# First attention's last blocks routed one by one, scatters spread, score weights multiplied ahead, experts' fetches reordered and tied to TensorE

## The reference, cut to what matters

```python
x = x + L0_xattn(layernorm(x), ctx, ctx, tokens, mask, ...)   # 16 heads, masked by equal tokens
x = x + L0_ffn(layernorm(x), router_w, w1, w2, expert_scale)  # top 2 of 8, silu
x = x + L1_xattn(layernorm(x), ctx, ...)                      # two directions, gated
x = x + L1_ffn(layernorm(x), Wg, bg, W1, W2, W3)              # top 2 of 8, capacity
```

## Time and profile before

| | |
|---|---|
| median of 3 runs | 1492.52 us (1490.99 to 1493.09) |
| the profiled execution's own time | 1491.39 us |
| its span, first to last instruction | 1489.5 us |
| mean granted TensorE clock | 0.957 of full |
| TensorE busy | 1356.2 us (91%) |
| VectorE / ScalarE / POOL busy | 850.7 / 817.5 / 667.9 us |
| first attention, TensorE's last count | 392 us |
| first experts, first matmul to last | 413.9 to 821.2 us |

### The profile page before, as it was taken

How to read it: one execution, slowest core, us unless ns; L and a number is a source line. 1 busy time by engine, 2 the same in 40 slices (tenths; PEclk the granted TensorE clock), 3 DMA queues, 4 the chain that set the end, 5 groups by cost and what they waited for, 6 DMA issues and landing times.

```text
span 1489.5 us, 37452 instructions
## 1 busy us (share of the span) xinstructions
PE 1356.2 (91%) x12922; PEld 1106.6 (74%) x12922; DVE 850.7 (57%) x2352; ACT 817.5 (55%) x1907; POOL 667.9 (45%) x936
## 2 busy tenths in 40 slices
PE   6999999997369999999999699999993999999996
PEld 5777777775226666666666699999982999999996
DVE  4787778887523222332232377777774566666664
ACT  4787777775135555554554355555552554454443
POOL 3234554554553333333310447777756444444322
PEclk8999999999579999999999899999996999999998
DMA  4343433432049999998897133333313433443331
GB/s 136 98 123 94 119 101 96 121 89 52 22 101 171 188 213 182 173 179 159 150 167 156 57 97 90 87 90 94 88 59 79 128 118 115 131 125 106 123 116 52
DMA packets 280856, 172.97 MB, mean 116 GB/s; under 512 B 212990, under 2 KB 259296, under 8 KB 280676
## 3 DMA queue, kind: packets, MB, share of 16 engines
q1 hardware_dynamic: 257940, 134.79, 39.7%
q0 software_dynamic: 18608, 32.21, 8.1%
q10 hardware_dynamic: 4128, 3.57, 0.9%
HBM read 93.44 MB, written 31.97 MB: 84 GB/s over the span
## 4 chain that ended last, share of the span: by engine, by line
PE 61%; DMA 3%; issue 3%; DVE 2%; ACT 2%; POOL 1%; another core or an unknown queue 1%; DVEq 0%; ACTq 0%; POOLq 0%; SPq 0%
PE psum L2308 14%; PE psum L1345 12%; PE psum L1358 12%; PE psum L2324 7%; PE psum L1828 4%; PE psum L1909 3%; PE psum L1834 3%; PE psum L1899 2%; DMA b_hT<-b_h 2%; PE psum L1875 1%; PE psum L1878 1%; DMA c_yg<-dram_expert_rows,c_gi 1%; ACT c_prT L1759 1%; PE psum L2292 1%
## 5 line engine op out<-in xcount | busy, mean ns | idle before, releaser
L1276 DVE SCALAR_TENSOR_TENSOR b_h<-b_hid,b_h 128x1024 f16<-128x1024 f32 x71 | 87.0, 1226 | 282.1 <-ACT b_h L1308 276.2
L2308 PE MATMUL psum<-d_xT,d_w 128*128 128x256 f16 (+1 forms) x2304 | 228.7, 256 | 0.0
L1345 PE MATMUL psum<-arena,b_xT 128*128 x852 | 200.8, 387 | 23.0 <-DMA b_xT<-b_x 21.6
L1358 PE MATMUL psum<-arena,b_hT 128*128 x1704 | 202.3, 276 | 13.1 <-DMA b_hT<-b_h 10.3
L2308 PEld LDWEIGHTS psum<-d_xT,d_w 128*128 128x128 f16 x2304 | 199.5, 98 | 19.3
L1358 PEld LDWEIGHTS psum<-arena,b_hT 128*128 128x128 f16 x1704 | 167.4, 99 | 52.2 <-issue 18.1
L1345 PEld LDWEIGHTS psum<-arena,b_xT 128*128 128x128 f16 x852 | 84.7, 100 | 114.9 <-issue 32.7
L1186 POOL DMA_INDIRECT b_xg<-dram_normed,b_gi x71 | 67.3, 948 | 207.4 <-DVE b_x L1269 195.6
L1303 ACT ACTIVATE b_hid<-psum 128x512 f32<-128x512 f32 x142 | 84.6, 597 | 137.5 <-PE psum L1345 99.2
L2368 ACT ACTIVATE d_sg<-psum 128x256 f32<-128x256 f32 (+1 forms) x192 | 65.9, 348 | 142.9 <-PE psum L2308 137.8
L2426 DVE SCALAR_TENSOR_TENSOR d_hf<-psum,d_sg 128x256 f32<-128x256 f32 (+1 forms) x192 | 71.2, 379 | 102.1 <-ACT d_sg L2368 86.1
(11 more groups left out here) (320 smaller groups left out, 2942.8 us busy)
## 6 DMA issues: line engine op xcount, KB each, us to landing
d_wst<-in_L_w SPq DMA_DIRECT2D x64, 384.0 KB
stage<-in_L_w SPq DMA_DIRECT2D x32, 512.0 KB
dram_expert_rows<-b_ys SPq DMA_DIRECT2D x71, 128.0 KB
ctxT<-in_ctxT SPq DMA_DIRECT2D x64, 128.0 KB
dram_normed<-xn SPq DMA_DIRECT2D x64, 128.0 KB
x<-in_x SPq DMA_DIRECT2D x32, 128.0 KB, 4.8
dram_x<-xnew SPq DMA_DIRECT2D x32, 128.0 KB
c_x<-dram_x SPq DMA_DIRECT2D x32, 128.0 KB
```

Of the source, the lines that this page charges most:

```text
L1276: dve.scalar_tensor_tensor(out=h16[:, p, 1, :], in0=hid[:, p, :], scalar=H_SCALE, in1=h16[:, p, 0, :], op0=ALU.mult, op1=ALU.subtract).the ...
L1345: i = pe.matmul(psum[:, 1 + 2 * p + half, :], xT[:, j % NT, px, c, :], weights(e, c, pw, half * 512, 512), start=(n == 0), stop=(n == len( ...
L1358: i = pe.matmul(psum[:, 6 + p, 0:D], hT[:, p, ph_, c, :], weights(e, 2 + c // 4, pw, (c % 4) * D, D), start=(n == 0), stop=(n == len(terms ...
L2308: i = pe.matmul(psum[:, q, m * n:(m + 1) * n], w16[:, fc % RING, pw, col:col + P], xT[:, p, px, c, at:at + n], start=(k == 0), stop=(k == ...
```

## The change

1. **Routing of the last blocks.** `GROUPS` ends in two groups of 2 (blocks 24 to 27) and four groups of 1 (28 to 31). The counts of these four go to another PSUM bank (`count_bank`). Their two factors (`probability`, `weights_out`) are made for all four at once (`WGROUPS`), after `tables`. In steps after 32 `slots_out` stands ahead of `top`.
2. **Scatters.** `scattered_at` gives 4 scatters to steps 30, 31 and 32 of POOL's loop where 3, 3 and 2 stood, and 2 each to steps 33, 34 and 35 where 2, 2, 2 and, in step 36, 4 stood.
3. **The fold** leaves the first experts. Its weights come by SP in the first attention; TensorE turns them in steps 32, 33 and 34 of the first attention (`turn_pe`), ScalarE copies them out (`turn_act`), and both multiply them between the two stages (`fold_pe`, `fold_act`). The results that second attention adds to its own weights are copied there by POOL (`scaled`), for which TensorE and VectorE wait at that stage's start (`c_cast`).
4. **Fetches.** POOL's loop of the first experts calls `gather(j)` ahead of `load_ids(j + 2)`, and `gather(j)` from j = 6 on also waits until `down(j - 6)` is done.
5. **Silu.** One `activation` of one column with Silu stands ahead of ScalarE's loop of the first experts.

```diff
-            GROUPS = [(b, RG) for b in range(0, NB - 2 * RG, RG)] + [(b, 2) for b in range(NB - 2 * RG, NB, 2)]
+            GROUPS = [(b, RG) for b in range(0, NB - 2 * RG, RG)] + [(b, 2) for b in range(NB - 2 * RG, NB - RG, 2)]
+            SINGLE = len(GROUPS)
+            WGROUPS = GROUPS + [(NB - RG, RG)]
+            GROUPS = GROUPS + [(b, 1) for b in range(NB - RG, NB)]
...
                     if n == RG and b < NB - 3 * RG:
                         return b + RG + 4
-                    if b < NB - 6:
-                        return NB - 4 + (2 * (b - NB + 3 * RG) + k) // 3
-                    return min(b + 6, NB + 4)
+                    if b < NB - 5:
+                        i = 2 * (b - NB + 3 * RG) + k
+                        return NB - 4 + (i // 3 if i < 6 else 2 + (i - 6) // 4)
+                    return min(b + 5, NB) if b < NB - RG else b + 4
...
+        def turn_pe(pe, k):
+            if k == 0:
+                pe.wait_ge(f_ld, 16 * (len(WN) + len(BN)))
+            t, bank = score_w[WN[k]], 3 + k
+            for o in range(DC):
+                for c in range(DC):
+                    i = pe.transpose(psum[:, bank, o * D + c * P:o * D + (c + 1) * P], t[:, c, o * P:(o + 1) * P], ident[:, :])
+            i.then_inc(turn_done, 1)
...
+            pe.wait_ge(turn_out, 2)
+            product(w["Wq_c"], w["Wk_s"], 3)
+            pe.wait_ge(turn_out, 4)
+            product(w["Wq_s"], w["Wk_c"], 4)
+            column(0, w["Wk_c"], bqs)
+            column(2, w["Wk_s"], bqc)
+            column(4, w["Wq_c"], bks)
+            column(6, w["Wq_s"], bkc)
+            dot(8, bqc, bks)
+            dot(9, bqs, bkc).then_inc(col_done, 1)
+
+        def fold_act(act):
+            act.wait_ge(col_done, 1)
+            act.activation(bm[:, :, :].rearrange("p d c -> p (d c)"), psum[:, 2, 0:4], ACT.Copy, scale=SC)
+            act.activation(consts[:, :], psum[:, 2, 4:10], ACT.Copy, scale=SC).then_inc(col_out, 1)
+            for k, t in enumerate((mc, ms)):
+                act.wait_ge(fold_done, k + 1)
+                act.activation(flat(t), psum[:, 3 + k, :], ACT.Copy).then_inc(fold_out, 1)
...
                 def gather(j):
                     if inside(j):
                         if due(j - NX + 1):
                             pool.wait_ge(xlo_ready, j - NX + 1)
+                            pool.wait_ge(down_done, j - NX + 1)
...
                 for j in range(N_B):
+                    gather(j)
                     load_ids(j + 2)
-                    gather(j)
...
+                act.activation(hid[:, 0, 0:1], xn2T[:, 0, 0:1], ACT.Silu)
                 for j in range(-4, N_B + 2):
...
             def scaled(pool):
                 pool.wait_ge(c_const, 16 * NL)
+                pool.wait_ge(col_out, 1)
+                for k, wt in enumerate((wvc, wvs)):
+                    pool.tensor_copy(wt[:, :, D:D + 1].rearrange("p c a -> p (c a)"), consts[:, 2 * k:2 * k + 2])
+                pool.tensor_copy(bv[:, :, D:D + 1].rearrange("p d a -> p (d a)"), consts[:, 4:6])
...
             @block.scalar
             def _(act):
                 a_act(act)
-                b_act(act, c_weights, c_fold_act)
+                fold_act(act)
+                b_act(act, c_weights)
...
             @block.tensor
             def _(pe):
                 a_pe(pe)
-                b_pe(pe, c_fold_pe)
+                fold_pe(pe)
+                b_pe(pe)
```

More of the change, by code:

```diff
@@ L207, in build @@
         x3_st, row_st = load_sems("x3_st"), sem("row_st")
-        kept = len(owned)
+        A_WORK = 61184
+        beside, in_wq = region(SHARED + WEIGHTS + A_WORK, WORK - A_WORK), region(SHARED + WEIGHTS + STAGED, 2048)
+        WN = ("Wq_c", "Wk_s", "Wq_s", "Wk_c")
+        BN = ("bqc", "bks", "bqs", "bkc")
+        score_w = {n: (in_wq if n == "Wk_c" else beside)("c_" + n, [P, DC, D]) for n in ("Wq_c", "Wq_s", "Wk_s", "Wk_c")}
+        score_b = beside("c_bqk", [P, len(BN), DC])
+        bm, consts = beside("c_bm", [P, 2, DC]), beside("c_consts", [P, 6])
@@ new lines, in build @@
+        f_ld, turn_done, turn_out, col_done, col_out, fold_done, fold_out = sem("f_load"), *(psem(f"f_{n}") for n in (
+            "turn", "turno", "col", "colo", "fold", "foldo"))
+        kept = len(owned)
+        SC = D ** -0.5
+        flat = lambda t: t[:, :, :].rearrange("p c d -> p (c d)")
+        bqc, bks, bqs, bkc = (score_b[:, i, :] for i in range(len(BN)))
+        mc, ms = score_w["Wq_c"], score_w["Wq_s"]
+        def turn_pe(pe, k):
[6 more added lines that the diff above has]
+            i.then_inc(turn_done, 1)
@@ new lines, in turn_act, with fold_pe, column, dot @@
+        def turn_act(act, k):
+            act.wait_ge(turn_done, k + 1)
+            act.activation(flat(score_w[WN[k]]), psum[:, 3 + k, :], ACT.Copy).then_inc(turn_out, 1)
+        def fold_pe(pe):
+            w = score_w
+            def column(at, wt, bias):
+                for k in range(DC):
+                    for o in range(DC):
+                        pe.matmul(psum[:, 2, at + k:at + k + 1], wt[:, o, k * P:(k + 1) * P], bias[:, o:o + 1], start=(o == 0), stop=(o == DC - 1))
+            def dot(at, x, y):
+                for o in range(DC):
+                    i = pe.matmul(psum[:, 2, at:at + 1], x[:, o:o + 1].to_broadcast([P, P]), y[:, o:o + 1], start=(o == 0), stop=(o == DC - 1))
+                return i
+            def product(wq, wk, bank):
+                for k in range(DC):
+                    for o in range(DC):
+                        i = pe.matmul(psum[:, bank, k * D:(k + 1) * D], wq[:, o, k * P:(k + 1) * P], wk[:, o, :], start=(o == 0), stop=(o == DC - 1))
+                i.then_inc(fold_done, 1)
+            pe.wait_ge(turn_out, 2)
[8 more added lines that the diff above has]
+            dot(9, bqs, bkc).then_inc(col_done, 1)
@@ L311, in last_of, with weights_of, place, count_bank @@
                 return g if j == n - 1 else None
+            def weights_of(b):
+                if b == NB - 1:
+                    return SINGLE
+                return last_of(b) if b < NB - RG else None
+            def place(g):
+                first, n = GROUPS[g]
+                o = max(0, g - SINGLE)
+                return o, o + n, min(g, SINGLE)
+            def count_bank(g):
+                return 0 if g >= SINGLE else 1
             def scattered(g, p):
@@ L863, in count @@
                     for j in range(n):
-                        i = pe.matmul(psum[:, 1, tot:tot + E], ones16[:, :], ghots16[:, j, :], start=(j == 0), stop=(j == n - 1))
+                        i = pe.matmul(psum[:, bank, tot:tot + E], ones16[:, :], ghots16[:, at + j, :], start=(j == 0), stop=(j == n - 1))
                     i.then_inc(cnt_done, 1)
@@ L985, in top @@
                         g, j, n = group_of[b]
+                        at, _, older = place(g)
                         if b == 0:
@@ L1262, in of_slots, with b_dve @@
                 dve.wait_ge(t_steps, k.next())
-            def b_dve(dve, fold):
+            def b_dve(dve):
                 def low_x(j):
@@ L1364, in b_pe @@
                     down(j - 1)
-                    fold(pe, j)
             def b_sync(sp, first_rows):
@@ L1453, in second_attention @@
             c_const, c_cast = sem("c_const"), psem("c_cast")
-            turn_done, turn_out, col_done, col_out, fold_done, fold_out = (psem(f"c_{n}") for n in ("turn", "turno", "col", "colo", "fold", "foldo"))
             yg_ld, x_ld, ctx_ld = load_sems("c_gather"), [sem(f"c_row{i}") for i in range(6)], load_sems("c_ctx")
```

250 lines of the change are left out of this document (99 added, 151 removed).

## The result

The changed kernel takes 1469.28 us (median of 4 runs, 1463.9 to 1472.17) against 1492.8 us (4 runs, 1490.99 to 1499.34): ratio 0.9837, 95% interval 0.9814 to 0.986, so 23.5 us less in the medians. The forecast was 1466.9, with a range of 1461 to 1478. The profiled execution took 1469.38 us (span 1467.6, granted clock 0.965), 22.0 us less than that of before.

The account below looks back on a forecast made before the run. TensorE was taken to bound the experts' steady part, waits the step into it. Gains 11.2 + 4.4 + 10.0 = 25.6 us from 1491.39 gave 1465.8, plus 1.1 for the median: 1466.9 us, range 1461 to 1478.

Parts of the forecast that it names:

- the hold: Behind up(0) in the first experts: ScalarE's 9.20 us wait without known releaser, expected to go with a shorter fetch run.
- the pieces put at nothing: Start to block 0's pT, attention blocks 0 to 31, and down(70) to the end: each forecast at 0.
- The fold leaves the experts: First experts' steady part: removing the fold's matmuls and the clock drop behind them saves 11.2 us.
- The matmuls' 9.45: First experts: the fold's turnings, bias groups and products take 9.45 us on TensorE's chain.
- the clock's 1.72: First experts: the up behind the longest bias group takes 4.31 us instead of 2.59, put down to one-column matmuls.
- The fold's new place: End of first attention and gap before up(0): fold hidden in waits, cost 0; ScalarE free at 405.6, deciding up(0).
- Routing and first fetch: Step from first attention into experts: earlier scatters, ids and rows; up(0) starts 4.4 us earlier, at 409.5.
- From `up(0)` to the steady part: Start of first experts, up(0) to down(1): 10.0 us gained, mostly if the hold goes with 14 fetches in the run.
- the hold stays: Rival behind up(0): the hold hangs on something other than the fetch run; gain 17.4 us, 1475.1 us; chance 0.16.
- The crowding rival: Rival in the experts' steady part: earlier gathers delay the turning of h (b_hT), 33 us lost, 1500 us; chance 0.04.
- The rule on instruction fetch: Sequencers fetch programs in 16 KiB blocks by DMA; by it a hold belongs to a program place, staying or moving.
- the rival of a place in the program: Instruction-fetch version of the hold staying, behind up(0): it stays or moves with the program, 1475.1 us; shares chance 0.16.

Follow-up runs that it names:

- the first pair: Kernel before and changed kernel as first measured, on a chip of the slower kind: 1492.8 and 1469.28 us, ratio 0.9837.
- experiment 5: The kernel before, unchanged, rerun and profiled on a chip of the faster (second) kind: 1461.75 us.
- Experiment 6: The changed kernel, unchanged, rerun on a chip of the faster (second) kind: 1444.74 us, ratio 0.9869 against the kernel before.
- Experiment 8: The changed kernel with the fold left out (no turnings, products, bias groups or ScalarE copies; bias terms zeroes, weights unfolded): 1450.08 us.
- experiment 10: The kernel before with only POOL's wait for down(j - 6) ahead of gather(j) added, on a slower (first kind) chip: 1484.88 us, ratio 0.9967.

## Why the prediction was right, and where not

The fold's move and its hiding went as forecast, and the hold went with the shorter run of fetches. The sum was 25.6 us forecast, 22.0 in the profiled pair, 23.5 in the medians. That the sum comes so near is in part luck: the three pieces to which it gave a gain gave 28.2 us, 2.6 more, and the pieces put at nothing took 6.3 back (-1.4, +3.6 and +4.1), for reasons that it didn't have. No run takes the new routing, the scatters or the order of fetches out alone, so the share of each in the step into the experts is read from the timelines. Step by step:

**The fold leaves the experts, 11.2.** Right in the first pair, where the steady part fell by 11.5. Over blocks 39 to 55 the time above 5.21 us a block fell from 11.6 to 0.7, so 10.9. The matmuls' 9.45 were never in doubt; the clock's 1.72 come in three of four traces with the fold there, at once behind the bias groups, but not in experiment 5. It is a likely cost and not a sure one. Between experiments 5 and 6 the steady part fell by only 7.2: over the same blocks the time above 5.21 us fell from 9.5 to 1.7, and the changed kernel lost some 4 us in two blocks behind a wait of 2.19 us for `b_hT` at 580.5, with a drop of the clock, where the unchanged one lost 2.4 in one block.

**The fold's new place, 0.** Right. The bias groups were forecast to be done at 402.6 and end at 402.57; ScalarE was to be free at 405.6 and is at 405.34. The clock rose in the middle of the products (3.76, then 2.06 us for the same eight matmuls) as in the sum. Experiment 8 shows no gain without the fold, in one profile. But I named the wrong gate: ScalarE waits for the rows.

**Routing and first fetch, 4.4.** 3.2 at `up(0)`, by two errors of opposite sign. From block 31 on the gain is 5.5 us, as my count for the rows alone had it (5.5); the last scatter ended at 396.36 (394.9 forecast), and of the 1.24 us for rows ahead of ids a part went into a wait for the ids to land (404.03, 0.81 us of idle). The error is the attention itself, which I took as unchanged: it became 3.6 us longer. On this kind of chip ScalarE's `pT` of block 30 waits 4.49 us instead of 2.98, with the run of scatters in that step grown from three to four and its end moved from 357.44 to 359.04. I had counted the scatters that the change takes from the end and not what a fourth one might do in steps 30 and 31. The longer wait explains 1.5 of the 3.6 us, and that the fourth scatter made it longer is read from the order in time; no run tests it. On the chip of experiments 5 and 6 this piece is +0.4 and the gain from block 31 on 8.0.

**From `up(0)` to the steady part, 10.0.** 11.2 in the pair. That the hold goes with the run of fetches is what experiment 10 shows, in one profile. What I didn't know is that it takes a certain chip. In no profile of the second kind is there a hold, and between experiments 5 and 6 this piece gives 1.0 instead. There the rival "the hold stays", at 17.4 us, gives the right total (17.6) by luck: nothing stays, since nothing was held.

What the hold is stays open, and "late signals" is too narrow a name for it. In the kernel before not only ScalarE stood still (its row is the last one here), but TensorE as well, inside the 24 matmuls of `down(0)`, which wait for no semaphore once they have begun:

```profile
433.51 0.27 PE L1358 MATMUL psum<-arena,b_hT 128*128 x1 [1.04 <-issue]
434.91 0.27 PE L1358 MATMUL psum<-arena,b_hT 128*128 x1 [1.13 <-issue]
435.62 0.96 PE L1358 MATMUL psum<-arena,b_hT 128*128 x6 [0.44 <-issue]
```
```profile
435.64 0.60 ACT L1303 ACTIVATE b_hid<-psum 128x512 f32<-128x512 f32 x1 [9.22 <-remote]
```

TensorE paused three times, 2.6 us in all, and ran on at 435.62, ScalarE at 435.64. POOL's last fetch had ended at 432.23. In experiment 10 and in the changed kernel `down(0)` has no such pause.

**The crowding rival** (1500). Not seen in the changed kernel: its steady part is 11.5 us shorter, and in the page's groups all the waits for `b_hT` of the stage are 6.0 us (busy time, mean ns of one, idle time before them):

```profile
L1473 PE MATMUL psum<-arena,b_hT 128*128 x1704 | 200.2, 275 | 6.0 <-DMA b_hT<-b_h 6.0
```
The Trainium skill ("DMA: Bandwidth & Descriptors", SWDGE vs HWDGE vs iDMA) says that a DMA engine serves GpSimd's and SP's transfers in turn, from queues of their own. The gather of 9.95 us in experiment 10, with `b_hT` late by 3.90, may be a case of transfers that get in each other's way, once and not in each block. The mechanism wasn't tested.

**The rule on instruction fetch.** I had used it for the rival of a place in the program. Experiment 5 has the same program without the hold, and experiment 10 loses it by a wait, so a fixed place doesn't explain it. The Trainium skill ("Runtime: NRT & Kernel Launch", instruction fetch mechanics) says that a sequencer fetches its program over a DMA queue of its own. Whether such a fetch was late while POOL's transfers ran, which would fit TensorE's pauses, no run here shows or rules out.

**What was given back** behind the first experts, 4.1 us in code that wasn't changed, wasn't in the forecast. 2.9 of it lie in the second experts (329.2 us against 326.3), mostly as five gaps of about 0.5 us, of which this is the first:

```profile
1182.37 0.22 PE L2343 MATMUL psum<-d_xT,d_w 128*128 128x128 f16 x1 [0.49 <-issue]
```

Experiment 6 has the same code with no gap of this length at this line, and the stage takes 324.2 us there. So the change alone isn't the cause; what is stays open.

Open as well: what tells the two kinds of chip apart, why engines stand still there, and whether the changed kernel without its pacing would be held on the first kind (tried three times, each time on a chip of the second).

## What to carry to other kernels

Take filler work out of a stage whose bound engine has no gaps and put it where that engine idles anyway: the sum of its matmuls was 9.45 us, and the stage became 7.2 to 11.5 us shorter without it, in three comparisons. Don't let GpSimd issue indirect DMAs far ahead in one unbroken run while other engines hand work to each other; pace them by the consumer. In the new order of fetches that had no cost that could be measured, and on one kind of chip the old order gained 4.9 us by it (0.7 to 9.1), 9.2 in the piece concerned. Before explaining a wait without a known releaser, run the unchanged kernel on another chip.

## What the runs showed of the hardware that I had not expected

- The same kernel takes 1462 us on one chip and 1492 us on another, with nearly the same mean granted clock (0.963 and 0.957). Of this, 16.4 us lie in blocks 0 to 31 of the first attention (340.24 against 323.80 us), and 10.2 between `up(0)` and `down(1)`. Blocks without scatters take the same time on both (10.30 us for blocks 2 to 6); among those with scatters some take 11.1 to 12.7 instead of 10.3 to 10.8.
- Part of that is TensorE's clock: in block 12 most of the scores' matmuls take 629 ns on the first kind, at 1.2 GHz, where they take 374 in block 11 at 2.4 GHz. Part is a late start of ScalarE: in blocks 29 and 30 it begins 2.5 us behind the start of the last group of scores (0.96 in most other blocks), 0.6 us after POOL's last scatter of the run ended; in the changed kernel it is 0.7 and 0.8 us after it.
- Fetches of 0.95 us at intervals of 1.25 were issued 29 in a row without a hold on the second kind, so the length of the run by itself is no measure of what it costs.
